# Two transformer blocks on one core: a row maximum taken from two neighbouring PSUM banks at once, score banks cut from three to two, and the products with the values moved into the middle of a step

## The chip, the cores and the metric

The kernel runs on one core of a Trainium2 chip. TensorE multiplies, VectorE, ScalarE and GpSimd work on what it makes, SyncE issues most transfers. TensorE writes into PSUM, which has eight banks of 512 float32 per partition; a bank can be written again when its reader is done. The metric is the device time of one execution in microseconds (us), taken as the median of several runs. Lower is better.

## The reference

Four sequences of 1024 tokens with 512 features pass two layers. Layer 0 is a block with conditioned layer norm, 16 heads of 32 with rotary embedding, and a feed-forward of 2048; layer 1 has 16 query heads on 4 key heads, no rotary, and gates. The heart of both:

```python
scores = jnp.einsum('bhqd,bhkd->bhqk', q, k) / np.sqrt(HD)
attn = jax.nn.softmax(scores, axis=-1)
out = jnp.einsum('bhqk,bhkd->bhqd', attn, v)
x = residual + out @ wo + bo
h = _ada_norm(x, cond, ln2_g, ln2_b, ada2_w, ada2_b)
ff = jax.nn.gelu(h @ ff_w1 + ff_b1, approximate=False) @ ff_w2 + ff_b2
return residual + ff
```

## The kernel before, in words

The program handles eight "batches" i in a row: the four sequences through layer 0 (i = 0 to 3), then through layer 1 (4 to 7). Each has an attention stage and a feed-forward stage. Each engine has its own instruction list, written out by hand, and the lists meet at counted semaphores.

An attention stage has 8 blocks (a group of four heads by 512 queries). Softmax needs each query's maximum over 1024 keys. It is computed ahead, in a pass of its own: for each of a block's 16 tiles (128 queries of one head), two matmuls of 512 keys ("halves", `max_item` of TensorE, L907) write a bank each, and VectorE reduces each bank to a column (L1476). After 32 halves a second small reduction joins the two columns of each tile (L1481), TensorE transposes them (L934), and a transfer puts them, negated, beside the queries as one more row, so that the later score matmul yields scores minus maximum. The maxima of block n + 1 are made while block n is used.

An attention stage is issued in 64 steps (8 for each block), followed by two steps that only finish. A step has
- four scores (`score`, L969): keys on partitions, 512 queries in a bank, which ScalarE turns into probabilities by an exponential (L1157);
- four halves of maxima for a later block, up to step 54 (there is no ninth block);
- the values (`values`, L986): four float32 matmuls with 32 columns of TensorE's array each (two passes, so eight instructions), over the probabilities of two steps earlier;
- in 30 of the steps, the totals (`totals`, L1001): the same form with ones, for the softmax's sums. Before it GpSimd adds two units of probabilities (`add_probs`, L702); an exponential waits until the sum that reads its slot six units earlier is done;
- in some steps a fill: a projection of keys, values or queries, an output projection, or a transpose for a layer norm.

Step s begins with a maximum; maxima and scores alternate; values and, where due, totals stand at the end (`attention` of TensorE, L1005). A score w goes to bank w modulo 3 and waits for exponential w - 3. Maxima and fills share banks 3, 6 and 7 in the attention stage, 6 and 7 elsewhere. A small planner at import (`pass_through`) deals them out: the least recently used allowed bank, whose next writer waits for the last reader (`bank_free`). Values accumulate in bank 4, totals in bank 5.

The last eight steps of an attention stage (the tail) have no maxima. The feed-forward has 33 iterations with 24 matmuls of 512 columns each (L806 to L808); from iteration 21 on, the next batch's first block of maxima is made between them. Before batch 0 there is a prologue, in which TensorE runs that same list of fills and maxima without a feed-forward around it.

ScalarE and VectorE also split weights into two half-precision parts in batches 0 to 3 (`split_high`, L1183, `split_low`, L1526), copy out the accumulated values and totals at fixed exponentials of a block (`O_AT`, `D_AT`), and finish a block two blocks later (`HI_AT`); GpSimd's part of it is placed by `LO_AT`.

## Time and profile before

| | |
|---|---|
| median of 3 runs | 4044.38 us (4036.17 to 4044.77) |
| the profiled execution | 4039.97 us, its span 4038.1 us |
| TensorE busy | 3800.2 us, 94% |
| VectorE busy | 2466.3 us, 61% |
| ScalarE busy | 1603.3 us, 40% |
| GpSimd busy | 1711.6 us, 42% |
| granted TensorE clock, mean | 0.975 |

The profile is that of one execution. A matmul's end is modelled and overlaps the next one's start, so the pace of TensorE is read from the distances of starts. A wait is put down to the instruction whose semaphore came last. "Granted clock" is the share of TensorE's full 2.4 GHz.

### The profile page before, as it was taken

What the parts mean: (1) busy time and instruction counts of PE and PEld (TensorE: products, weight loads), DVE (VectorE), ACT (ScalarE), POOL (GpSimd) and SP (SyncE); (2) the same over time, 40 slices, a digit from 0 to 9 for tenths busy, and PEclk for the clock granted to TensorE, in tenths of its full rate; (3) what the DMA queues carried; (4) which work ended last, traced back from release to release, by engine and by line L of the source; (5) the groups of instructions that cost most, each with busy time, mean ns of one, the idle gap of its engine ahead of it and who ended that gap; (6) DMA issues with size and microseconds to landing.
All of it is one profiled execution on the core that took longest, in us unless ns stands there. A gap on an engine that the chain in (4) does not pass through costs nothing.

```text
span 4038.1 us, 53506 instructions
## 1 busy us (share of the span) xinstructions
PE 3800.2 (94%) x20400; PEld 1502.4 (37%) x20400; DVE 2466.3 (61%) x3903; ACT 1603.3 (40%) x2807; POOL 1711.6 (42%) x955
## 2 busy tenths in 40 slices
PE   6988899998999989999899998999899998999999
PEld 4322344333543335433254323432244333533244
DVE  4687645765457755576555777367664776467742
ACT  1365312653125632155421653136511563136521
POOL 2376412673216742066510664037510673126620
PEclk9899999999999999999999999999999999999999
DMA  4232243212423223332233022311222112311122
GB/s 143 52 99 91 97 106 86 71 54 82 107 78 81 59 74 89 100 82 59 85 100 94 17 62 69 111 40 25 82 80 90 30 38 79 113 53 25 61 66 94
DMA packets 138973, 305.21 MB, mean 76 GB/s; under 512 B 19632, under 2 KB 59588, under 8 KB 137824
## 3 DMA queue, kind: packets, MB, share of 16 engines
q10 hardware_dynamic: 50944, 174.62, 13.4%
q1 hardware_dynamic: 87776, 127.17, 12.1%
q8 instruction: 164, 2.69, 0.3%
q14 instruction: 89, 0.73, 0.1%
HBM read 223.46 MB, written 36.66 MB: 64 GB/s over the span
## 4 chain that ended last, share of the span: by engine, by line
PE 80%; DVE 9%; POOL 4%; issue 3%; ACT 3%; DMA 1%; SPq 0%; ACTq 0%; POOLq 0%; DVEq 0%
PE ps L806 12%; PE ps L807 12%; PE ps L808 12%; PE ps L986 10%; PE ps L907 9%; PE ps L969 8%; PE ps L843 7%; PE ps L1001 5%; DVE mcol L1476 3%; PE ps L860 2%; POOL sums L702 2%; ACT probs L1157 2%; DVE ring L1526 2%; PE ps L824 1%; DVE dcopy L1493 1%
## 5 line engine op out<-in xcount | busy, mean ns | idle before, releaser
L702 POOL TENSOR_TENSOR sums<-probs 128x1024 f32<-128x1024 f32 x496 | 1175.6, 2384 | 1039.5 <-PE ps L1001 570.0
L1476 DVE TENSOR_REDUCE mcol<-ps 128x1 f32<-128x512 f32 x2048 | 1289.4, 682 | 454.0 <-PE ps L907 451.6
L1157 ACT ACTIVATE probs<-ps 128x512 f32<-128x512 f32 x2048 | 1098.9, 607 | 854.0 <-PE ps L969 617.6
L907 PE MATMUL ps<-ks,qs 97*128 97x512 f16 x2048 | 790.6, 388 | 64.4 <-DVE mcol L1476 47.0
L969 PE MATMUL ps<-qs,ks 98*128 98x512 f16 x2048 | 776.6, 389 | 77.4 <-ACT probs L1157 73.0
L1302 ACT ACTIVATE sums<-ps,cols 128x512 f32<-128x512 f32 x256 | 175.9, 687 | 1153.9 <-PE ps L808 1153.9
L986 PE MATMUL ps<-probs,v_sb 128*32 128x512 f32 x4096 | 568.0, 631 | 0.0
L907 PEld LDWEIGHTS ps<-ks,qs 97*128 97x128 f16 x2048 | 199.7, 98 | 624.9 <-DVE mcol L1476 375.2
L806 PE MATMUL ps<-ring,probs 128*128 128x512 f16 x1024 | 390.8, 382 | 20.6 <-DVE probs L1572 20.6
L806 PE MATMUL ps<-aT,ring 128*128 128x512 f16 x1024 | 388.3, 379 | 6.5 <-ACT dcopy L1169 6.5
L807 PE MATMUL ps<-ring,probs 128*128 128x512 f16 x1024 | 390.3, 381 | 0.0
L808 PE MATMUL ps<-ring,probs 128*128 128x512 f16 x1024 | 389.9, 381 | 0.0
L807 PE MATMUL ps<-aT,ring 128*128 128x512 f16 x1024 | 388.2, 379 | 0.0
L808 PE MATMUL ps<-aT,ring 128*128 128x512 f16 x1024 | 388.0, 379 | 0.0
L969 PEld LDWEIGHTS ps<-qs,ks 98*128 98x128 f16 x2048 | 198.0, 98 | 381.2 <-ACT probs L1157 247.5
L1571 DVE CAST probs<-sums 128x512 f16<-128x512 f32 x256 | 132.9, 519 | 305.7 <-ACT sums L1302 305.7
L843 PE MATMUL ps<-hT,wqkv 128*128 128x512 f16 x1248 | 297.3, 382 | 5.2 <-DVE wqkv L1646 5.2
L1001 PE MATMUL ps<-sums,ones 128*32 128x512 f32 x2048 | 280.6, 621 | 0.0
L687 POOL TENSOR_TENSOR turn<-turn 128x512 f32<-128x512 f32 x32 | 41.0, 1281 | 548.5 <-DVE turn L1410 548.5
L1572 DVE TENSOR_TENSOR probs<-sums,probs 128x512 f16<-128x512 f32 x256 | 207.4, 810 | 8.8
L1410 DVE SCALAR_TENSOR_TENSOR turn<-ps,bias,trig 128x512 f32<-128x512 f32 x128 | 89.9, 746 | 166.0 <-PE ps L843 149.7
L843 PEld LDWEIGHTS ps<-hT,wqkv 128*128 128x128 f16 x1248 | 120.8, 98 | 161.1 <-DVE mcol L1476 11.1
(106 smaller groups left out, 3273.7 us busy)
## 6 DMA issues: line engine op xcount, KB each, us to landing
ring<-halves ACTq DMA_DIRECT2D x208, 512.0 KB, 3.4
qs<-hl SPq DMA_DIRECT2D x192, 128.0 KB, 4.0
ring<-halves SPq DMA_DIRECT2D x48, 512.0 KB, 6.4
ring<-in_weights ACTq DMA_DIRECT2D x39, 512.0 KB, 4.3
halves<-ring ACTq DMA_DIRECT2D x37, 512.0 KB, 2.9
ks<-hl SPq DMA_DIRECT2D x120, 128.0 KB, 4.4
dcopy<-inverses SPq DMA_DIRECT2D x56, 256.0 KB
probs<-in_x SPq DMA_DIRECT2D x8, 1024.0 KB, 6.9
```

The source lines that it names most:

```text
L702: pool.tensor_tensor(sums[:, m % SUM_SLOTS, :, :], prob(u - 2), prob(u), ALU.add).then_inc(sum_set[0].sem, 1)
L806: pe.matmul(dst, lhs[0], rhs[0], start=first, stop=False)
L807: pe.matmul(dst, lhs[0], rhs[1], start=False, stop=False)
L808: return pe.matmul(dst, lhs[1], rhs[0], start=False, stop=last)
L843: mm = pe.matmul(bank, qkv(lw, weight_at(kind, i, hh, part, c), P), hT[:, lx, c, tok], start=(q == 0), stop=(q == 11))
L907: pe.matmul(bank, qs[0:K_MAX, hh, h, P * qt:P * qt + P], ks[0:K_MAX, key_set(i, hh), key_head(i, hh, h), 512 * half:512 * half + 512], sta ...
L969: pe.matmul(ps[:, bank, :], ks[0:K_EXP, key_set(i, hh), key_head(i, hh, h), P * kt:P * kt + P], qs[0:K_EXP, hh, h, :], start=True, stop=Tr ...
L986: mm = pe.matmul(ps[32 * q:32 * q + 32, 4, :], values_of(i, hh)[:, kt, value_cut(i, hh, 4 * g + q)], prob(u + q // 2)[:, q % 2, :], start= ...
L1001: mm = pe.matmul(ps[32 * q:32 * q + 32, 5, :], ones32[:, :], sums[:, (m + q // 2) % SUM_SLOTS, q % 2, :], start=(m % 8 == 0), stop=(m % 8 ...
L1157: act.activation(prob(u)[:, e, :], ps[:, w % SCORE_BANKS, :], ACT.Exp).then_inc(exp_done.sem, 1)
L1476: dve.tensor_reduce(mcol[:, blk % 2, 4 * j + qt, half:half + 1], src, AX.X, ALU.max).then_inc(n_free[0], 1)
L1572: dve.tensor_tensor(fT[:, n % 4, 1, :], g32[:, n % 2, :], fT[:, n % 4, 0, :], ALU.subtract).then_inc(f_set.sem, 1)
```

## The change

- Two halves of a tile go to two neighbouring banks, and VectorE takes one maximum over 1024 keys from both. The second small reduction and its buffer go. A block has 16 items of two halves; two items are issued in a step, as four halves were.
- The banks: scores 2 (0 and 1) instead of 3; maxima and fills 2, 3, 6, 7. An item takes a pair, (2, 3) or (6, 7); a fill takes a single bank of the four. In the feed-forward stage and the prologue there is only the pair (6, 7). Two banks, 2 and 3, now pass between the attention stage and the outputs of the feed-forward.
- In a step TensorE's order becomes: half 0, score 0, half 1, values, score 1, (first part of a fill), score 2, (second part), halves 2 and 3, score 3, and totals at the end where due.
- Small moves: the copy of totals from exponential 12 to 11 of a block, the finish from 11 to 15, GpSimd's part of it from sum 1 to 3; the parts of a weight split one to two exponentials or one step later, its store later too; one rotation's high part.
- In the feed-forward two items an iteration from 21 on (one from 27 on), the first ahead of the second matmul of the feed-forward, the other behind it.

```diff
@@ -30,19 +30,20 @@
 SCORES = 2 * UNITS
-SCORE_BANKS, MAX_BANKS, LATER_BANKS = 3, (3, 6, 7), (6, 7)
+SCORE_BANKS, MAX_BANKS, LATER_BANKS = 2, (2, 3, 6, 7), (6, 7)
+PAIRS = (2, 6)
 LAG = 4
 PROBS, SUM_SLOTS, SUMS = 6, 3, 64
-O_AT, D_AT, HI_AT, INVERT_AT, NORM_AT, LO_AT = 7, 12, 11, 4, 6, 1
+O_AT, D_AT, HI_AT, INVERT_AT, NORM_AT, LO_AT = 7, 11, 15, 4, 6, 3
 RING = 6
...
 L0_CHUNKS, L1_CHUNKS = 24, 21
-MAX_AT = (4, 6, 8, 10, 12, 14, 16, 18, 20, 22, 24, 26, 28, 30, 32)
-MAX_AT_K = (0, 2, 5, 7, 9, 11, 14, 16, 18, 20, 23, 25, 27, 29, 32)
+MAX_AT = (2, 4, 6, 8, 10, 12, 14, 16)
+MAX_AT_K = (0, 2, 4, 7, 9, 11, 14, 16)
 WO_AT = 52
...
 BIAS_AT = (49, 49, 50, 51, 53, 54, 55, 56)
-TURNS = ((("k", 1, 0), -1, 1, 5), (("k", 1, 1), 3, 3, 10), (("q", 0, 1), 11, 13, 29), (("q", 1, 1), 25, 27, 57))
+TURNS = ((("k", 1, 0), -1, 1, 5), (("k", 1, 1), 3, 3, 11), (("q", 0, 1), 11, 13, 29), (("q", 1, 1), 25, 27, 57))
@@ -54,19 +55,20 @@
-def max_step(i, u):
-
-    blk, s = divmod(u, 16)
-    if s < 14:
+def maxima_at(i, s):
+
+
+    blk, r = divmod(s, 8)
+    if r < 7:
         at = MAX_AT_K if layer(i) == 0 and blk == 1 else MAX_AT
-        items = [(blk + 1, k) for k in range(at[s], at[s + 1])]
+        items = [(blk + 1, k) for k in range(at[r], at[r + 1])]
     else:
-        items = [] if layer(i) == 0 and blk == 0 else [(blk + 2, k) for k in range(2 * (s - 14), 2 * (s - 13))]
-    return [(n, k) for n, k in items if n < 8]
+        items = [] if layer(i) == 0 and blk == 0 else [(blk + 2, k) for k in range(2)]
+    return [("max", i, n, k) for n, k in items if n < 8]
...
 def max_tile(k):
-    return k // 2 % 4, k // 8, k % 2
+    return k % 4, k // 4
@@ -141,13 +139,13 @@
         keys += [key for at, key in first_fills(j) if at == n]
-        first = {21: 0, 22: 4, 23: 8, 24: 11, 25: 14, 26: 17, 27: 20, 28: 23, 29: 26, 30: 29}
+        first = {21: 0, 22: 2, 23: 4, 24: 6, 25: 8, 26: 10, 27: 12, 28: 13, 29: 14, 30: 15}
         if n in first:
-            keys += [("max", j, 0, k) for k in range(first[n], first.get(n + 1, 32))]
+            keys += [("max", j, 0, k) for k in range(first[n], first.get(n + 1, 16))]
+        if n in (31, 32):
+            keys += [("max", j, 1, n - 31)]
         if n == 31:
             keys += [("rows", j, 0)]
-        if n in (31, 32):
-            keys += [("max", j, 1, 2 * (n - 31)), ("max", j, 1, 2 * (n - 31) + 1)]
     return keys
@@ -171,31 +169,45 @@
+
 NARROW, BANK, USER_BEFORE, FREED, LAST_USER = {}, {}, {}, {}, {}
...
 def pass_through(key, banks):
-    bank = [b for b in recent_ if b in banks][0]
-    recent_.remove(bank)
-    recent_.append(bank)
-    NARROW[key], BANK[key], USER_BEFORE[key] = len(NARROW), bank, LAST_USER.get(bank)
-    LAST_USER[bank] = key
+    if key[0] == "max":
+        _, bank = min((max(recent_.index(b), recent_.index(b + 1)), b) for b in PAIRS if b in banks)
+        used = (bank, bank + 1)
+    else:
+        bank = [b for b in recent_ if b in banks][0]
+        used = (bank,)
+    before = []
+    for b in used:
+        recent_.remove(b)
+        recent_.append(b)
+        if b in LAST_USER and LAST_USER[b] not in before:
+            before.append(LAST_USER[b])
+        LAST_USER[b] = key
+    NARROW[key], BANK[key], USER_BEFORE[key] = len(NARROW), bank, before
     read_[by_scalar(key)] += 1
...
-THIRD_FIRST, THIRD_LAST = {}, []
+SHARED_FIRST, SHARED_LAST = {}, []
 for i_ in range(-1, NB):
...
         keys_ = [key_ for s_ in range(STEPS) for key_ in narrow_attention(i_, s_)]
+        first_, last_ = {}, {}
         for key_ in keys_:
             pass_through(key_, MAX_BANKS)
-        third_ = [key_ for key_ in keys_ if BANK[key_] == 3]
-        THIRD_FIRST[third_[0]] = i_
-        THIRD_LAST.append(third_[-1])
+            for b_ in (2, 3):
+                if LAST_USER.get(b_) == key_:
+                    first_.setdefault(b_, key_)
+                    last_[b_] = key_
+        SHARED_FIRST.update({key_: i_ for key_ in first_.values()})
+        SHARED_LAST.append(list(dict.fromkeys(last_.values())))
     for n_ in range(FC * 2 + 1):
@@ -808,11 +818,10 @@
             def bank_free(key):
-                before = USER_BEFORE[key]
-                if before is not None:
+                for before in USER_BEFORE[key]:
                     pe.wait_ge(*freed(before))
-                if key in THIRD_FIRST and THIRD_FIRST[key] >= 1:
-                    pe.wait_ge(y_read.sem, y_read.at(THIRD_FIRST[key]))
+                if SHARED_FIRST.get(key, 0) >= 1:
+                    pe.wait_ge(y_read.sem, y_read.at(SHARED_FIRST[key]))
                 return ps[:, BANK[key], :]
@@ -896,17 +905,28 @@
-            def max_item(key):
+            def max_item(key, half):
+
                 _, i, blk, k = key
                 hh, qc, g = block_of(blk)
-                if k == 0:
-                    stacks_ready(i, blk)
-                bank = bank_free(key)
-                j, qt, half = max_tile(k)
+                if half == 0:
+                    if k == 0:
+                        stacks_ready(i, blk)
+                    bank_free(key)
+                j, qt = max_tile(k)
                 h = 4 * g + j
-                pe.matmul(bank, qs[0:K_MAX, hh, h, P * qt:P * qt + P],
-                          ks[0:K_MAX, key_set(i, hh), key_head(i, hh, h), 512 * half:512 * half + 512],
-                          start=True, stop=True).then_inc(n_full, 1)
+                mm = pe.matmul(ps[:, BANK[key] + half, :], qs[0:K_MAX, hh, h, P * qt:P * qt + P],
+                               ks[0:K_MAX, key_set(i, hh), key_head(i, hh, h), 512 * half:512 * half + 512],
+                               start=True, stop=True)
+                if half == 1:
+                    mm.then_inc(n_full, 1)
+
+            def max_halves(keys):
+                return [(key, half) for key in keys for half in range(2)]
+
+            def some_halves(halves):
+                for key, half in halves:
+                    max_item(key, half)
@@ -930,13 +950,13 @@
                 bank = bank_free(key)
-                pe.wait_ge(max_col.sem, max_col.at(i, blk + 1))
-                pe.transpose(bank[0:16, 0:P], mfin[:, :], ident[:, :]).then_inc(n_full, 1)
+                pe.wait_ge(*freed(("max", i, blk, 15)))
+                pe.transpose(bank[0:16, 0:P], mcol[:, blk % 2, :], ident[:, :]).then_inc(n_full, 1)
...
                 if kind == "max":
-                    max_item(key)
+                    some_halves(max_halves([key]))
                 elif kind == "rows":
@@ -1005,24 +1025,24 @@
                     u = 2 * s
+                    halves, fills = max_halves(maxima_at(i, s)), FILLS[i].get(s, [])
                     if s < STEPS:
-                        maxima, fills = maxima_at(i, s), FILLS[i].get(s, [])
-                        some(maxima[0:1])
+                        some_halves(halves[0:1])
                         score(i, 4 * s)
-                        some(maxima[1:2])
+                        some_halves(halves[1:2])
+                    if LAG <= u < UNITS + LAG:
+                        values(i, u - LAG)
+                    if s < STEPS:
                         score(i, 4 * s + 1)
...
                             fill(key, 0, 6 if key[0] in "kqv" else 12)
-                        some(() if fills else maxima[2:3])
                         score(i, 4 * s + 2)
...
                                 fill(key, 6, 12)
-                        some(maxima[2:3] if fills else maxima[3:4])
+                        some_halves(halves[2:4])
                         score(i, 4 * s + 3)
-                        some(maxima[3:] if fills else maxima[4:])
-                    if LAG <= u < UNITS + LAG:
-                        values(i, u - LAG)
+                        some_halves(halves[4:])
                     if s == STEPS + 1:
@@ -1061,7 +1081,8 @@
                             pe.wait_ge(exp_done.sem, exp_done.at(i, SCORES))
-                            pe.wait_ge(*freed(THIRD_LAST[i]))
+                            for key in SHARED_LAST[i]:
+                                pe.wait_ge(*freed(key))
                         for t in range(4):
@@ -1268,9 +1287,9 @@
                     for q, (st, ch) in enumerate(here):
-                        if u == 2 * st:
+                        if u == 2 * st + 1:
                             split_high(i, q)
-                        if u == 2 * st + 4:
+                        if u == 2 * st + 7:
                             store_split(i, q)
@@ -1471,14 +1490,14 @@
                 _, i, blk, k = key
-                j, qt, half = max_tile(k)
-                src = bank_full(key)
-                dve.tensor_reduce(mcol[:, blk % 2, 4 * j + qt, half:half + 1], src, AX.X, ALU.max).then_inc(n_free[0], 1)
+                j, qt = max_tile(k)
+                bank_full(key)
+                src = ps[:, BANK[key]:BANK[key] + 2, :].rearrange("p a d -> p (a d)")
+                at_ = 4 * j + qt
+                dve.tensor_reduce(mcol[:, blk % 2, at_:at_ + 1], src, AX.X, ALU.max).then_inc(n_free[0], 1)
...
                 _, i, blk = key
-                dve.wait_ge(*freed(("max", i, blk, 31)))
-                dve.tensor_reduce(mfin[:, :], mcol[:, blk % 2, :, :], AX.X, ALU.max).then_inc(max_col.sem, 1)
                 src = bank_full(key)
@@ -1549,9 +1568,9 @@
                     for q, (st, ch) in enumerate(here):
-                        if s == st:
+                        if s == st + 1:
                             split_low(i, q, 0)
-                        if s == st + 1:
+                        if s == st + 2:
                             split_low(i, q, 1)
...
```

TensorE in step 40 of batch 4, before: L907 is a half of a maximum, L969 a score, L986 the values, L1001 the totals; in brackets what each waits for (exp_done: exponentials; n_free: VectorE's reader).

```order
L907 MATMUL ps<-ks,qs 128x512 [waits n_free]
L969 MATMUL ps<-qs,ks 128x512 [waits exp_done,max_in]
L907 MATMUL ps<-ks,qs 128x512 [waits n_free]
L969 MATMUL ps<-qs,ks 128x512 [waits exp_done]
L907 MATMUL ps<-ks,qs 128x512 [waits n_free]
L969 MATMUL ps<-qs,ks 128x512 [waits exp_done]
L907 MATMUL ps<-ks,qs 128x512 [waits n_free]
L969 MATMUL ps<-qs,ks 128x512 [waits exp_done]
L986 MATMUL ps<-probs,v_sb 32x512 [waits exp_done]
L986 MATMUL ps<-probs,v_sb 32x512 x3
L1001 MATMUL ps<-sums,ones 32x512 [waits sum_set0]
L1001 MATMUL ps<-sums,ones 32x512 x3
```

The same step after; L918 is a half, L989 a score, L1006 the values, L1021 the totals.

```order
L918 MATMUL ps<-ks,qs 128x512 [waits n_free]
L989 MATMUL ps<-qs,ks 128x512 [waits exp_done,max_in]
L918 MATMUL ps<-ks,qs 128x512
L1006 MATMUL ps<-probs,v_sb 32x512 [waits exp_done]
L1006 MATMUL ps<-probs,v_sb 32x512 x3
L989 MATMUL ps<-qs,ks 128x512 [waits exp_done] x2
L918 MATMUL ps<-ks,qs 128x512 [waits n_free]
L918 MATMUL ps<-ks,qs 128x512
L989 MATMUL ps<-qs,ks 128x512 [waits exp_done]
L1021 MATMUL ps<-sums,ones 32x512 [waits sum_set0]
L1021 MATMUL ps<-sums,ones 32x512 x3
```

The values have moved from before the totals to behind the first score, so the step has two places with 32-column matmuls, and the second half of an item waits for nothing.

TensorE at the end of the prologue, before: value projections (L860), the 32 halves of block 0, the transpose (L934), and the first halves of block 1.

```order
L860 MATMUL ps<-wqkv,hT 128x256 [waits n_free,s_rows]
L860 MATMUL ps<-wqkv,hT 128x256 x23
L907 MATMUL ps<-ks,qs 128x512 [waits mask_in0,stack_in0,n_free]
L907 MATMUL ps<-ks,qs 128x512 [waits n_free] x31
L934 MATMUL ps<-ident,mfin 16x128 [waits max_col,n_free]
L907 MATMUL ps<-ks,qs 128x512 [waits mask_in0,stack_in0,n_free]
L907 MATMUL ps<-ks,qs 128x512 [waits n_free] x3
```

The same place after (L869 is the projection, L918 a half):

```order
L869 MATMUL ps<-wqkv,hT 128x256 [waits n_free,s_rows]
L869 MATMUL ps<-wqkv,hT 128x256 x23
L918 MATMUL ps<-ks,qs 128x512 [waits mask_in0,n_free,stack_in0]
L918 MATMUL ps<-ks,qs 128x512
L918 MATMUL ps<-ks,qs 128x512 [waits n_free]
L918 MATMUL ps<-ks,qs 128x512
L918 MATMUL ps<-ks,qs 128x512 [waits n_free]
```

Every second half is now preceded by a wait for a reader; all these items have the one pair of banks 6 and 7, where before two single banks were filled in turn.

## Rows read from the trace of the kernel before

**Rows 1.** The page, part 1: busy us, share of the span, instructions.
```profile
PE 3800.2 (94%) x20400; PEld 1502.4 (37%) x20400; DVE 2466.3 (61%) x3903; ACT 1603.3 (40%) x2807; POOL 1711.6 (42%) x955
```

**Rows 2.** TensorE's waits: us, times, longest; whole run, then batch 0 (129:436).
```profile
PE ps L969 <- ACT probs L1157: 73.0, 110, 9.0
PE ps L907 <- DVE mcol L1476: 47.0, 59, 2.2
...
PE ps L934 <- DVE mfin L1481: 10.2, 17, 1.8
...
PE ps L907 <- DVE mcol L1476: 20.7, 15, 2.2
```

**Rows 3.** Windows (batch 4, steps 40-47; tail): us; busy PE, PEld, DVE, ACT, POOL; clock.
```profile
2353.40:2380.20 26.80, 26.51 (x163) 7.97 (x162) 20.72 (x35) 18.12 (x36) 21.06 (x11) 1.00 0.03 11
2415.40:2453.00 37.60, 29.13 (x158) 8.44 (x160) 21.56 (x22) 21.20 (x41) 20.98 (x12) 0.86 0.24 89
```

**Rows 4.** Timeline of TensorE, batch 4, steps 37 and 38: start, duration.
```profile
2342.73 1.04 PE L1001 MATMUL ps<-sums,ones 128*32 128x512 f32 x8
2343.70 0.39 PE L907 MATMUL ps<-ks,qs 97*128 97x512 f16 x1
...
2345.24 0.38 PE L969 MATMUL ps<-qs,ks 98*128 98x512 f16 x1
2345.55 1.06 PE L986 MATMUL ps<-probs,v_sb 128*32 128x512 f32 x8
2346.55 0.39 PE L907 MATMUL ps<-ks,qs 97*128 97x512 f16 x1
...
2348.39 1.06 PE L986 MATMUL ps<-probs,v_sb 128*32 128x512 f32 x8
2349.28 1.04 PE L1001 MATMUL ps<-sums,ones 128*32 128x512 f32 x8
2350.25 0.28 PE L934 MATMUL ps<-ident,mfin 128*16 128x128 f32 x1
```

**Rows 5.** The same stretch on ScalarE, GpSimd and VectorE.
```profile
2346.42 3.04 ACT L1157 ACTIVATE probs<-ps 128x512 f32<-128x512 f32 x6 [0.99 <-POOL sums L702]
...
2343.95 4.67 POOL L702 TENSOR_TENSOR sums<-probs 128x1024 f32<-128x1024 f32 x2 [0.75 <-PE ps L1001]
...
2344.13 2.48 DVE L1476 TENSOR_REDUCE mcol<-ps 128x1 f32<-128x512 f32 x4 [0.77 <-PE ps L907]
```

**Rows 6.** Tail of batch 2: timeline of TensorE, then of ScalarE.
```profile
1435.23 0.82 PE L969 MATMUL ps<-qs,ks 98*128 98x512 f16 x3
1436.31 0.39 PE L969 MATMUL ps<-qs,ks 98*128 98x512 f16 x1 [0.26 <-ACT probs L1157]
...
1445.56 0.61 PE L969 MATMUL ps<-qs,ks 98*128 98x512 f16 x1 [3.59 <-ACT probs L1157]
...
1435.66 2.07 ACT L1157 ACTIVATE probs<-ps 128x512 f32<-128x512 f32 x4 [0.45 <-PE ps L969]
...
1444.91 1.08 ACT L1157 ACTIVATE probs<-ps 128x512 f32<-128x512 f32 x2 [4.21 <-POOL sums L702]
```

**Rows 7.** The page, part 5: draining a rotated projection on VectorE.
```profile
L1410 DVE SCALAR_TENSOR_TENSOR turn<-ps,bias,trig 128x512 f32<-128x512 f32 x128 | 89.9, 746 | 166.0 <-PE ps L843 149.7
```

**Rows 8.** Timeline of ScalarE in batch 2: a split of weights.
```profile
1278.05 1.09 ACT L1183 ACTIVATE ring<-ring 128x1024 f16<-128x1024 f32 x1
```

**Rows 9.** Timeline of TensorE in the prologue.
```profile
106.97 1.21 PE L907 MATMUL ps<-ks,qs 97*128 97x512 f16 x2 [0.18 <-DVE mcol L1476]
108.36 1.21 PE L907 MATMUL ps<-ks,qs 97*128 97x512 f16 x2 [0.18 <-DVE mcol L1476]
```

18 lines of the change are left out of this document (6 added, 12 removed).

## The prediction

> **What bounds the kernel now.** I read the page's busy times first: TensorE is busy 94% of the span, VectorE 61% and ScalarE 40% [rows 1]. Its waits sum to little: 73.0 us for exponentials (ScalarE has not yet emptied a score bank), 47.0 us for maxima (VectorE), 10.2 us for the small reduction ahead of the row transposes [rows 2]. The windows then show where they lie. Steps 40 to 47 of batch 4 last 26.8 us, with TensorE busy 26.51 us at full clock; the last eight steps, which have no maxima, last 37.6 us with 29.13 us busy, at a clock of 0.86 [rows 3]. So seven eighths of an attention stage of the second layer run at the rate at which TensorE issues, and there a change can only lose; what can be gained lies in the tails, in batch 0 (20.7 us of waits for maxima, [rows 2]) and a little in batches 1 to 3.
>
> "Busy" hides short waits, since a 0.38 us matmul overlaps the next, which starts 0.22 us later. So the pace is read from starts [rows 4]. An odd step lasts 2343.70 to 2346.55 = 2.85 us: four scores and four maxima in turn, seven distances of (2345.24 - 2343.70)/7 = 0.22, then 0.31 from the last score to the values and 1.00 from the values to the next matmul. An even step lasts to 2350.25 = 3.70 us: values to totals 0.89, totals onward 0.97. A pair is 6.55 us.
>
> **1. Values in mid-step: one more switch.** Before, values and totals of an even step are neighbours. A matmul of 128 columns is followed by the next after 0.22, but by values after 0.31; values are followed by totals after 0.89, but by a half-precision matmul after 1.00 [rows 4]. With values between score 0 and score 1, and totals still at the end, each even step has both edges twice: 0.09 + 0.11 = 0.20 us more. The order rows show the two separate visits. 30 totals per batch stand in steps, 240 in all, so 48 us if nothing hides it; the five per batch that lie in the waiting tail count for nothing here. The Trainium skill, TensorEngine Tiling (Array Packing), Key Properties, says that a change of tiling mode drains TensorE; values and totals are 32-column tiles. The trace agrees that each such edge costs, and it is a rule against this change; the sum takes 0.20 us from the rows.
>
> **2. Two score banks.** Score w now waits for exponential w-2, not w-3. A score at 1435.23 has its exponential at 1435.66, 0.43 later; the fourth score from there waited for the first one's bank and started at 1436.31, 0.65 after that exponential [rows 6]. So two scores of one bank cannot start closer than 1.08 us. Before, three banks asked this of scores six matmuls (1.3 us) apart. After, score 1 and score 3 have only score 2 and two halves between them, 4 x 0.22 = 0.88: a wait of 0.20 in every step without a fill, which holds up all that stands behind it on TensorE (totals, the next item), and through it VectorE and ScalarE, which idle there. Score 0 and score 2 have the values between them and are safe.
> Score 0 of the next step needs the exponential of score 2. GpSimd decides that one after a step with totals: totals at 2342.73, exponential released by the sum at 2346.42, 3.69 later [rows 4, 5], bank free at 4.34. The score is due at 0.97 + odd step 3.05 + 0.22 = 4.24: a wait of 0.10. Here 3.05 = 0.22 + 0.22 + 0.31 + 1.00 + 1.08 + 0.22.
> The even step becomes 0.22 + 0.22 + 0.31 + 1.00 + 1.08 + 0.31 + 0.97 = 4.11. The pair is 4.11 + 3.05 + 0.10 = 7.26 against 6.55: +0.71, in which the switch of part 1 is contained. None of it shows as much idle time: waits of 0.1 to 0.2 us lie under the modelled 0.38 us.
> Steps 2 to 51 without a fill: 46 in each batch of layer 1, 38 in batches 1 to 3, 40 in batch 0, together 338, or 169 pairs. 169 x 0.71 = **120 us**. Its bounds: 34 us (169 x 0.20, if waits for score banks vanish under other waits) and 135 us (0.80 a pair, if ScalarE is late as well). I take 120, since batch 4's rows leave nothing else to hide it.
> Outside those pairs 31 switches in fill steps add 31 x 0.20 = +6 us. In tails the same two-bank rule gives an odd step without maxima 0.31 + 1.00 + 1.08 + 0.48 = 2.87 (0.48: the second exponential starts half a microsecond behind the first); before, 0.31 + 1.00 + 3 x 0.22 = 1.97 was possible. But the tail waits for GpSimd: one of its sums let an exponential through at 1444.91 only, and TensorE waited 3.59 us [rows 6]. TensorE's slower steps mostly eat that wait: +5 us for eight batches (0 to +25).
>
> **3. One maximum over 1024 keys.** 2048 reductions of 0.68 us (four in 2.48 us back to back, so 0.60 each, [rows 5]) become 1024. One of twice the length costs between 0.68 and 1.20; I take 1.20, as the time should grow with the elements. VectorE loses little work; what counts is the bank cycle: the reduction starts about 0.43 after the second half, ends 1.20 later. In the attention two pairs alternate, an item per pair and step, against steps of 3 us: no wait. In the feed-forward only banks 6 and 7, one pair, are left, but 2.6 us of matmuls stand between items: no wait either. Two places lack that cover.
> The prologue issues 16 items in a row. Before: pairs of halves every 1.39 us (106.97 to 108.36), the pace of VectorE [rows 9]. After, TensorE writes two halves, waits for the whole reduction and starts again: 0.22 + 0.43 + 1.20 + 0.05 = 1.9 us at full clock, and about 2.4 with matmuls at twice the distance, as this stretch seems to have them (its matmuls last 0.61 us on average where others last 0.38). 16 x (2.3 - 1.39) = +15 us (8 to 20). And in step 21 of the feed-forward ahead of batches 1 to 3 a value projection and two items come in one run behind each other on that pair: 3 x 2.4 = +7 us.
> A fill takes a bank of the pair that the next step's first item needs, with 4 x 0.22 of cover in an odd step instead of 2 us; its drain takes 0.43 plus two operations of 0.75 [rows 7]. About 1 us in seven fill steps of each early batch and two of each late one, less about as much that batches 0 to 3 already wait: +12 us.
>
> **4. ScalarE's and VectorE's other work.** Splits of weights (1.09 us each on ScalarE, [rows 8]), the two-part finishes of a block and the copies now stand at other exponentials and meet one bank less of cover. A split between two exponentials delays the second by 1.1 us, and score 2, two places behind it, has 1.75 us less 1.08 to spare: 39 splits and 24 finishes at 0.2 us on average: +12 us (0 to 25). First steps 0 and 1 of a batch: +5 us.
> On the other side the splits' second halves move a step later on VectorE, and it no longer waits for ScalarE between reductions. I give back 30 of the 47.0 us of waits for maxima, 5 of the 10.2 us ahead of the row transposes, as that reduction is gone [rows 2], and 5 us of clock in batch 0: -40 us.
>
> **Sum.** 120 + 6 + 5 + 15 + 7 + 12 + 12 + 5 - 40 = +142 us on the profiled execution's 4040.0 us: 4182. The runs' median is 4.4 us above that execution: **4186 us**, 3.5% slower.
>
> **The rivals.**
> A. The short waits are hidden after all (exponentials sooner than the two rows say, or the score wait overlaps the array switch), and only the switches cost: 34 + 6 for them, and the other terms as they are: 120 becomes 34, +56 us, 4100. For it: no row of before has a score whose bank was used two scores ago. Against: the 0.43 and 0.65 are the way from score to exponential and back, whichever bank it is.
> B. The idle slivers bring the clock down. The tail of batch 4, busy 77%, ran at 0.86 [rows 3]. If the 338 steady steps ran at 0.95 instead of 1.00, their 169 x 7.26 = 1227 us would grow by 5%: +65 us more, 4251. Against: in the new pair TensorE waits only 0.50 of 7.26 us. The Trainium skill, TensorE: Matmul & The Clock Gate, A second HAM failure mode, describes this of PSUM banks cycled with small idles; no row here shows it in the steady steps.
> C. Faster. Values issued ahead of scores 1 to 3 free the probability slots earlier, VectorE is no longer late, and TensorE stops waiting for both: all 73.0 + 47.0 + 10.2 us go [rows 2] and two-bank waits do not appear, against 48 us of switches: -82 us, 3962. It decides if exponentials in the tails are released by values, not by GpSimd's sums. Against: the releaser of the long wait is the sum [rows 6], and the steady steps have nothing to give.
> D. Gains and losses cancel within 0.2% (8 us, about what a measurement of this kernel can tell from no change): 4044.
>
> **How the numbers follow.** The forecast has 0.72, A 0.12, B 0.09, C 0.04, D 0.03. Slower: 0.72 + 0.12 + 0.09 = 0.93; same 0.03, faster 0.04. The range must leave out no more than 0.2: with the bounds of the terms (the tail, prologue, fills and ScalarE's other work together -25 to +45 around the sum, the 120 down to 34) it is 4095 to 4265, which holds A and nearly B.
>
> **What would show it.** In the steady steps of batch 4: pairs of about 7.2 us by starts; values 0.31 after a maximum and 1.00 ahead of score 1; score 3 at 1.08 after score 1, its wait put down to ScalarE; totals with edges 0.31 and 0.97; the block of steps 40 to 47 near 29.5 us instead of 26.8, clock 1.00. The reduction near 1.2 us, 1024 of them. Prologue items 1.9 to 2.4 us apart. Fewer waits for maxima in batch 0. It would be wrong if steady pairs stay below 6.9 us, if the clock sinks there, or if the tails get shorter by more than a few us.

## The result: slower by 4.9%, and the profile after

The changed kernel takes 4238.05 us (median of 4 runs, 4235.68 to 4244.49) against 4043.1 us for the kernel before (median of 4 on the same chip): a ratio of 1.0488 (95% interval 1.0470 to 1.0506). The forecast was 4186 us, 3.5% slower, in a range of 4095 to 4265. The profiled execution took 4235.68 us, its span 4233.9, so 195.8 us more of span than before. The direction is as forecast and the time lies in the range, but the loss is 195 us where 142 were forecast.

The page of the changed kernel, engines and its longest reduction (L1497 is the maximum):

```profile
PE 3915.0 (92%) x20400; PEld 1444.2 (34%) x20400; DVE 2415.9 (57%) x2815; ACT 1680.1 (40%) x2807; POOL 1721.0 (41%) x955
...
L1497 DVE TENSOR_REDUCE mcol<-ps 128x1 f32<-128x1024 f32 x1024 | 1238.4, 1221 | 709.9 <-PE ps L918 708.9
```

TensorE's waits (L989 a score, L918 a half, L1006 the values, L954 the row transpose; us in total, times, longest), to be read beside [rows 2]:

```profile
PE ps L989 <- ACT probs L1176: 98.7, 142, 4.2
PE ps L954 <- DVE mcol L1497: 30.8, 27, 2.0
PE ps L918 <- DVE mcol L1497: 29.2, 25, 1.4
PE ps L1006 <- ACT ocopy L1182: 20.8, 43, 0.6
...
PE ps L918 <- DVE turn L1429: 17.1, 20, 0.9
...
PE ps L918 <- DMA ks<-hl: 8.8, 4, 2.8
PE ps L918 <- DVE hl L1438: 7.4, 8, 1.2
```

VectorE is less busy than before (2415.9 us), as intended, and TensorE waits longer. The ones for exponentials rose from 73.0 to 98.7 us and the ones ahead of the row transposes by 20.6, those for maxima fell from 47.0 to 29.2; most of the loss is not in this list. It is in the starts. Windows of batch 4, steps 40 to 47 and the tail, beside [rows 3]:

```profile
2463.70:2493.90 30.20, 29.34 (x162) 6.78 (x163) 20.23 (x19) 19.52 (x36) 21.21 (x11) 1.00 0.03 11
2531.00:2571.40 40.40, 31.86 (x168) 8.09 (x167) 20.91 (x23) 23.25 (x42) 21.88 (x13) 0.87 0.23 83
```

The block of eight steps went from 26.8 to 30.2 us at full clock, with 29.34 us "busy". The clock did not sink there, and on the whole it is 0.975 as before. TensorE's timeline there, steps 36 and 37 and the start of 38, beside [rows 4]:

```profile
2448.42 0.38 PE L918 MATMUL ps<-ks,qs 97*128 97x512 f16 x1
2448.73 0.39 PE L989 MATMUL ps<-qs,ks 98*128 98x512 f16 x1
2448.96 0.38 PE L918 MATMUL ps<-ks,qs 97*128 97x512 f16 x1
2449.27 1.06 PE L1006 MATMUL ps<-probs,v_sb 128*32 128x512 f32 x8
2450.27 0.61 PE L989 MATMUL ps<-qs,ks 98*128 98x512 f16 x2
2450.71 0.60 PE L918 MATMUL ps<-ks,qs 97*128 97x512 f16 x2
2451.35 0.39 PE L989 MATMUL ps<-qs,ks 98*128 98x512 f16 x1
2451.66 1.06 PE L1021 MATMUL ps<-sums,ones 128*32 128x512 f32 x8
2452.66 0.39 PE L918 MATMUL ps<-ks,qs 97*128 97x512 f16 x1
...
2455.72 0.38 PE L918 MATMUL ps<-ks,qs 97*128 97x512 f16 x1
2456.04 0.39 PE L989 MATMUL ps<-qs,ks 98*128 98x512 f16 x1
```

The reader is to see four distances. Values 0.31 after a half and 1.00 ahead of score 1 (2449.27, 2450.27); score 3 at 2451.35, exactly 1.08 after score 1, 0.20 behind where it could have stood; totals again 0.31 and 1.00; and at the start of step 38 the score at 2456.04, 0.32 instead of 0.22 after its half, the 0.10 us that GpSimd's late sum costs. From first score to first score the even step is 4.16, the odd one 3.14 to 3.15 us: a pair of 7.30, where 7.26 was forecast and 6.55 stood.

### The profile page after: what moved, and what is told of

Read it like the earlier page. It is cut to its first block, busy times and chain, and to the rows that moved or that the text cites. A ratio compares the mean times of both kernels' runs of the same rounds, so it can differ in the third digit from the quotient of the medians.

```text
span 4233.9 us, 52561 instructions
## 1 busy us (share of the span) xinstructions
PE 3915.0 (92%) x20400; PEld 1444.2 (34%) x20400; DVE 2415.9 (57%) x2815; ACT 1680.1 (40%) x2807; POOL 1721.0 (41%) x955
## 4 chain that ended last, share of the span: by engine, by line
PE 80%; DVE 7%; ACT 5%; POOL 4%; issue 3%; DMA 1%; ACTq 0%; SPq 0%; POOLq 0%; DVEq 0%
PE ps L816 12%; PE ps L818 11%; PE ps L817 11%; PE ps L989 10%; PE ps L1006 10%; PE ps L918 9%; PE ps L852 6%; PE ps L1021 5%; ACT probs L1176 3%; POOL sums L712 2%; DVE mcol L1497 2%; PE ps L869 2%; PE ps L833 1%; DMA ks<-hl 1%; DVE turn L1429 1%
## 5 line engine op out<-in xcount | busy, mean ns | idle before, releaser
L1497 DVE TENSOR_REDUCE mcol<-ps 128x1 f32<-128x1024 f32 x1024 | 1238.4, 1221 | 709.9 <-PE ps L918 708.9
L1176 ACT ACTIVATE probs<-ps 128x512 f32<-128x512 f32 x2048 | 1167.6, 596 | 935.8 <-PE ps L989 878.2
L989 PE MATMUL ps<-qs,ks 98*128 98x512 f16 x2048 | 747.3, 394 | 113.7 <-ACT probs L1176 98.7
L918 PE MATMUL ps<-ks,qs 97*128 97x512 f16 x2048 | 701.3, 389 | 81.2 <-DVE mcol L1497 29.2
L1006 PE MATMUL ps<-probs,v_sb 128*32 128x512 f32 x4096 | 561.5, 622 | 22.5 <-ACT ocopy L1182 20.8
L989 PEld LDWEIGHTS ps<-qs,ks 98*128 98x128 f16 x2048 | 173.5, 97 | 896.0 <-ACT probs L1176 736.6
L816 PE MATMUL ps<-ring,probs 128*128 128x512 f16 x1024 | 391.1, 382 | 20.6 <-DVE probs L1591 20.6
L918 PEld LDWEIGHTS ps<-ks,qs 97*128 97x128 f16 x2048 | 200.3, 99 | 425.8 <-DVE mcol L1497 148.3
L1021 PE MATMUL ps<-sums,ones 128*32 128x512 f32 x2048 | 280.7, 621 | 0.0
L852 PEld LDWEIGHTS ps<-hT,wqkv 128*128 128x128 f16 x1248 | 122.4, 98 | 151.7 <-issue 10.2
```

Source lines behind the costliest of these rows:

```text
L816: pe.matmul(dst, lhs[0], rhs[0], start=first, stop=False)
L852: mm = pe.matmul(bank, qkv(lw, weight_at(kind, i, hh, part, c), P), hT[:, lx, c, tok], start=(q == 0), stop=(q == 11))
L918: mm = pe.matmul(ps[:, BANK[key] + half, :], qs[0:K_MAX, hh, h, P * qt:P * qt + P], ks[0:K_MAX, key_set(i, hh), key_head(i, hh, h), 512 * ...
L989: pe.matmul(ps[:, bank, :], ks[0:K_EXP, key_set(i, hh), key_head(i, hh, h), P * kt:P * kt + P], qs[0:K_EXP, hh, h, :], start=True, stop=Tr ...
L1006: mm = pe.matmul(ps[32 * q:32 * q + 32, 4, :], values_of(i, hh)[:, kt, value_cut(i, hh, 4 * g + q)], prob(u + q // 2)[:, q % 2, :], start= ...
L1021: mm = pe.matmul(ps[32 * q:32 * q + 32, 5, :], ones32[:, :], sums[:, (m + q // 2) % SUM_SLOTS, q % 2, :], start=(m % 8 == 0), stop=(m % 8 ...
```

## Where the 195 us lie

Differences of the starts of scores, summed by kind of step over all batches (measured in both traces), against what the terms of the forecast gave to the same places. A tail is counted from the first score of step 56 to its last score; what follows, up to the next batch's first score, stands under the feed-forward stages.

| place | forecast | measured |
|---|---|---|
| steps without a fill, from the third to step 51 | 120 + 12 - 40 = 92 | 108.2 |
| steps with a fill (32.3), and 52 to 55 (14.2) | 6 + 12 = 18 | 46.5 |
| prologue | 15 | 15.3 |
| first two steps of a batch (batches 4 to 7 alone: 7.9) | 5 | 7.3 |
| tails | 5 | 10.4 |
| feed-forward stages | 7 | 8.0 |
| sum | 142 | 195.7 |

The first line by batches: batches 4 to 7 lose 76.5 us, batches 1 to 3 lose 36.2, and batch 0 gains 4.5.

## Experiments

Twelve kernels. A name that begins with b_ is the kernel before with an edit, one with a_ the changed kernel with an edit. Ratios are to the kernel before on the same chip. The changed kernel was timed on the chip of the result alone, where the kernel before took 4043.1 us; on the three chips of the experiments that took 4035.8 to 4037.7. So "faster than the changed kernel" is the difference of two losses, each against the kernel before on its own chip: 195 us for the changed kernel. The plain difference of the two medians is 5 to 7 us more.

### 1. Values in mid-step alone

```diff
 # TensorE, attention: kernel before
                         some(maxima[1:2])
+                    if LAG <= u < UNITS + LAG:
+                        values(i, u - LAG)
+                    if s < STEPS:
                         score(i, 4 * s + 1)
...
                         some(maxima[3:] if fills else maxima[4:])
-                    if LAG <= u < UNITS + LAG:
-                        values(i, u - LAG)
```

> The kernel before, with the values issued between the first and the second score of a step; three score banks, single banks for maxima. Theory (each separate visit of the 32-column matmuls costs about 0.20 us, 240 totals stand in steps): the even step of the second layer goes from 3.70 to 3.90 us, the odd one stays at 2.85, the whole is 40 to 48 us slower, about 4087 us. Rival (the switch is hidden, or values issued earlier free something): no change or faster, 4043 us or less.

Measured 4128.05 us, 1.0227 (1.0213 to 1.0241): +90 us, twice the forecast of the switch. TensorE in steps 37 and 38 of batch 4:

```profile
2392.01 0.39 PE L907 MATMUL ps<-ks,qs 97*128 97x512 f16 x1
...
2392.45 0.38 PE L907 MATMUL ps<-ks,qs 97*128 97x512 f16 x1
2392.76 1.06 PE L986 MATMUL ps<-probs,v_sb 128*32 128x512 f32 x8
2393.76 0.39 PE L969 MATMUL ps<-qs,ks 98*128 98x512 f16 x1
...
2395.30 0.38 PE L907 MATMUL ps<-ks,qs 97*128 97x512 f16 x1
```

The switch is what was forecast: the odd step is 2.85 (from the matmul ahead of the values, 2392.45, to the same one of the next step, 2395.30), the even one 3.94 against 3.70, +0.24, which over 200 steps is 48 us. The rest shows up in waits that the move uncovers (TensorE's waits in this kernel), beside [rows 2]:

```profile
PE ps L986 <- ACT ocopy L1164: 65.1, 44, 5.5
...
PE ps L934 <- DVE mfin L1482: 28.5, 25, 1.9
PE ps L969 <- ACT probs L1158: 23.7, 16, 9.3
...
PE ps L907 <- DVE turn L1411: 20.4, 24, 0.9
```

The values wait for the copy of their bank, 65.1 us in 44 waits; no such wait stood in the list of before. Not all of that is loss: 33.7 us of it are eight single waits, one in each tail, and the tails became 10 us shorter, as the waits for exponentials fell from 73.0 to 23.7 us. The row transposes wait 28.5 instead of 10.2 us, and a first maximum behind a rotated projection 20.4 us. At the end of a step the values' 1.3 us (0.31 and 1.00) had stood in front of all three. By steps: those with a fill lose 34.8 us and steps 52 to 55 another 20.1, their switches included. The theory of the switch stands, the theory that the switch is all falls.

### 2. Two score banks alone

```diff
-SCORE_BANKS, MAX_BANKS, LATER_BANKS = 3, (3, 6, 7), (6, 7)
+SCORE_BANKS, MAX_BANKS, LATER_BANKS = 2, (3, 6, 7), (6, 7)
```

> The kernel before with two score banks in turn instead of three (bank 2 idle in the attention stage), all else as before. Theory (two scores of one bank start at least 1.08 us apart, and the second exponential follows the first by 0.48): score 2 at 1.08 instead of 0.88 after score 0, score 3 at 1.56 instead of 1.32, so every steady step is 0.24 us longer, 2.85 to 3.09 and 3.70 to 3.94; 338 steps give +81 us, about 4125 us. Rival (the waits for score banks vanish under others): within 10 us of before.

Measured 4132.85 us, 1.0231 (1.0217 to 1.0245): +95 us. The steady steps of batch 4 are 3.14 odd and 3.96 even (3.09 and 3.94 expected), with one of 3.59 a block. They carry 77.5 of the 95 us; steps with fills and 52 to 55 lose 1.4 us together. This kernel's list of waits understates it:

```profile
PE ps L969 <- ACT probs L1157: 106.7, 169, 8.8
```

That is 34 us more than before, for a loss of 95: the remainder lies under the modelled ends of matmuls. The rival is out. Alone, the moved values and the two banks cost about 2.3% each; the whole change costs 4.9%.

### 3. Values back at the end of the step, two banks kept

```diff
 # TensorE, attention: changed kernel
                         some_halves(halves[1:2])
-                    if LAG <= u < UNITS + LAG:
-                        values(i, u - LAG)
-                    if s < STEPS:
                         score(i, 4 * s + 1)
...
                         some_halves(halves[4:])
+                    if LAG <= u < UNITS + LAG:
+                        values(i, u - LAG)
```

> The changed kernel with the values back at the end of a step, next to the totals; two score banks and the pairs stay. Theory (mid-step values cost a switch but cover a score bank): the second visit goes (-0.20 us in an even step), but score 2 now follows score 0 with 0.66 us between and must keep 1.08, so each step waits 0.42. By starts in the second layer's steady steps 3.27 odd and 4.12 even, a pair of 7.39 us against 7.28: that alone +19 us. The waits that appeared behind fills and ahead of the row transposes (values no longer cover VectorE) should go at the same time: about 1 us in seven fill steps of batches 0 to 3 and two to four of the others, and 0.2 to 0.5 us a block: -30 us. About 4225 us, 4205 to 4260. Rival (the switch is all that the move costs): pairs of 7.08 us and 4190 us or less.

Measured 4205.18 us, 1.0423 (1.0407 to 1.0439), 26 us faster than the changed kernel, twice the 13 expected. The steady steps came as worked out, 3.27 odd and 4.12 to 4.13 even (3.27 and 4.12 expected): worse than with values in mid-step. One even step a block takes 4.50, which nothing here explains. What got better is the steps with fills (-24.1 us) and 52 to 55 (-7.2). This time the waits for exponentials show in the list, as a steady step should wait 0.42 us:

```profile
PE ps L989 <- ACT probs L1175: 205.5, 424, 4.0
```

So with two banks values in mid-step are the better place in a steady step, and the worse one in a step with a fill. The rival (pairs of 7.08) is out.

### 4. Another order for the same two banks

```diff
+                    spaced = s < STEPS and halves and not fills and not rows_at(i, s)
                     if s < STEPS:
-                        some_halves(halves[0:1])
+                        some_halves([] if spaced else halves[0:1])
                         score(i, 4 * s)
-                        some_halves(halves[1:2])
+                        some_halves(halves[0:2] if spaced else halves[1:2])
+                        if spaced:
+                            score(i, 4 * s + 1)
                     if LAG <= u < UNITS + LAG:
                         values(i, u - LAG)
+                    for pair in range(SUMS // 2 - 2):
+                        if spaced and s == totals_step(i, pair):
+                            totals(i, 2 * pair)
                     if s < STEPS:
-                        score(i, 4 * s + 1)
+                        if not spaced:
+                            score(i, 4 * s + 1)
...
-                        if s == totals_step(i, pair):
+                        if not spaced and s == totals_step(i, pair):
                             totals(i, 2 * pair)
```

> The changed kernel, but steps that have maxima and neither a fill nor a row transpose are issued as score 0, half, half, score 1, values, totals, score 2, half, half, score 3. Theory (only distances between scores of one bank and visits of the 32-column matmuls set the pace): score 0 to 2 and 1 to 3 are covered by the values, score 2 to the next score 0 has 0.88 and needs 1.08, one visit an even step: odd 3.05, even 3.91 us, the pair 6.96 instead of 7.28; a block of steps 32 to 39 of the second layer about 28.5 instead of 30.1 us; 4180 us, 4170 to 4195. Rival (the number of score banks as such sets the pace, by ScalarE): pairs stay at 7.2 or more and the whole within 15 us of the changed kernel.

Measured 4161.97 us, 1.0308 (1.0294 to 1.0323), 69 us faster than the changed kernel; the time is below the 4170 to 4195 expected. The steps of batch 4 from 32 on: 3.89, 3.05, 4.16, 3.05, 3.91, 3.07, 4.08, 3.30, together 28.5 us, as forecast to the tenth. Step 36 and the start of 37:

```profile
2422.84 1.07 PE L1006 MATMUL ps<-probs,v_sb 128*32 128x512 f32 x8
2423.73 1.04 PE L1021 MATMUL ps<-sums,ones 128*32 128x512 f32 x8
2424.70 0.39 PE L989 MATMUL ps<-qs,ks 98*128 98x512 f16 x1
2424.93 0.60 PE L918 MATMUL ps<-ks,qs 97*128 97x512 f16 x2
2425.36 0.81 PE L989 MATMUL ps<-qs,ks 98*128 98x512 f16 x2
2426.01 0.60 PE L918 MATMUL ps<-ks,qs 97*128 97x512 f16 x2
```

Values and totals touch (0.89), one visit; score 2 at 2424.70, and the next score 0 is the second of the two from 2425.36, held by its bank until about 1.08 after score 2. The number of banks sets the pace only through the distance between two scores of one bank; the rival is out.

### 5. The length of the maximum

```diff
-                src = ps[:, BANK[key]:BANK[key] + 2, :].rearrange("p a d -> p (a d)")
+                src = ps[:, BANK[key]:BANK[key] + 2, :].rearrange("p a d -> p (a d)")[:, ::2]
...
-                dve.tensor_scalar(mT[:, :], src[0:16, 0:P], -1.0, None, ALU.mult).then_inc(n_free[0], 1)
+                dve.tensor_scalar(mT[:, :], src[0:16, 0:P], -1.0, -40.0, ALU.mult, ALU.add).then_inc(n_free[0], 1)
```

> The changed kernel with the maximum taken over every second of the 1024 keys only (half of the keys left out of the maximum, and 40 subtracted to keep the exponentials small), so that the instruction has 512 elements, as long as one of before. Theory (of the whole loss the length of the maximum is the small part: it delays the prologue's items, the row transposes and a few first maxima): reduction 0.68 us instead of 1.22, prologue 10 us shorter, the row transposes' 30.8 us and the maxima's 29.2 us of waits smaller by 20 us together; 25 to 35 us faster than the changed kernel, about 4208 us, and the steady pair still 7.28 us. Rival (the longer reduction is what slows the steady steps): pairs near 6.75 us and under 4120 us.

Measured 4197.74 us, 1.0397 (1.0383 to 1.0411), 34 us faster than the changed kernel. The steady pair did not move (4.15 and 3.14 us); the prologue is 8.9 us shorter, and of TensorE's waits the two for the maximum, 29.2 and 30.8 us in the changed kernel, are here

```profile
PE ps L918 <- DVE mcol L1497: 20.5, 30, 0.9
...
PE ps L954 <- DVE mcol L1497: 11.3, 17, 1.1
```

The longer reduction costs about a sixth of the loss, and nothing in the pairs that have neither fill nor transpose. The rival is out.

### 6. The prologue

```diff
-            pass_through(key_, LATER_BANKS)
+            pass_through(key_, LATER_BANKS if i_ >= 0 else MAX_BANKS)
```

> The changed kernel with both pairs of banks open to the prologue as well, where it has only the pair (6, 7). Theory (with one pair TensorE writes and VectorE reduces in turn, 2.3 us an item; with two they overlap, about 1.2 to 1.4 us an item): attention of batch 0 starts 12 to 16 us earlier and the whole is 12 to 16 us faster, about 4224 us. Rival (VectorE or the clock bounds the prologue): under 5 us.

Measured 4217.83 us, 1.0440 (1.0426 to 1.0454), 15 us faster. In the changed kernel, items follow each other after 2.35 us, beside [rows 9], and VectorE is busy for 1.22 of it only. Its TensorE (the distance of two items):

```profile
106.59 1.03 PE L918 MATMUL ps<-ks,qs 97*128 97x512 f16 x2 [1.32 <-DVE mcol L1497]
108.94 1.03 PE L918 MATMUL ps<-ks,qs 97*128 97x512 f16 x2 [1.32 <-DVE mcol L1497]
```

VectorE between them, in the same kernel:

```profile
107.66 1.22 DVE L1497 TENSOR_REDUCE mcol<-ps 128x1 f32<-128x1024 f32 x1 [1.13 <-PE ps L918]
```

TensorE in the experiment, with both pairs:

```profile
106.75 2.17 PE L918 MATMUL ps<-ks,qs 97*128 97x512 f16 x4 [0.19 <-DVE mcol L1497]
109.10 2.17 PE L918 MATMUL ps<-ks,qs 97*128 97x512 f16 x4 [0.19 <-DVE mcol L1497]
```

Four halves, two items, in 2.35 us. The first score comes 25.6 us earlier (12 to 16 expected). Of these, 17.6 us are the items themselves, now 1.18 us apart, VectorE's pace. Another 7.0 us lie ahead of them: the edit opens the banks to the prologue's projections too, and the first item starts at 95.3 instead of 102.3. About 10 of the 25.6 us are lost again later, mostly in attention steps (7 us); why stays open.

### 7. The copy of the values

The changed kernel, and the kernel before:

```diff
-O_AT, D_AT, HI_AT, INVERT_AT, NORM_AT, LO_AT = 7, 11, 15, 4, 6, 3
+O_AT, D_AT, HI_AT, INVERT_AT, NORM_AT, LO_AT = 6, 11, 15, 4, 6, 3
```

```diff
-O_AT, D_AT, HI_AT, INVERT_AT, NORM_AT, LO_AT = 7, 12, 11, 4, 6, 1
+O_AT, D_AT, HI_AT, INVERT_AT, NORM_AT, LO_AT = 8, 12, 11, 4, 6, 1
```

> The changed kernel with the copy of the accumulated values after exponential 6 of the next block instead of 7. Theory (43 waits of 0.48 us of the values for that copy, 20.8 us, exist because the values moved ahead of three scores while the copy did not move): these waits go, the step at s mod 8 = 2 falls from 4.74 to about 4.2 us, the whole by 15 to 22 us, to 4218 us. Rival (the copy ahead of exponential 7 delays it and with it a score by as much): within 6 us.

> The kernel before with the same copy after exponential 8 instead of 7. In its trace the step at s mod 8 = 2 takes 4.17 us instead of 3.70, since exponential 8, released late by GpSimd's sum, stands behind the copy, and score 3 waits for its bank. Theory: with the exponential first that wait shrinks to 0.1 us, 0.35 us in some 48 steps: -15 us, 4028 us. Rival (the values then wait for the copy by as much): within 4 us of before.

Measured 4219.87 us, 1.0455 (1.0439 to 1.0471), 11 us faster than the changed kernel (its span is 17 us shorter; 15 to 22 expected): the step at s mod 8 = 2 went from 4.74 to 4.20, and the 20.8 us of waits are gone but for 0.2. For the kernel before: 4027.91 us, 0.9980 (0.9971 to 0.9989): that step of the kernel before fell from 4.17 to 3.93 only, half of the forecast's gain.

### 8. The splits of weights

In the kernel before, the moves of the change; in the changed kernel, their undoing.

```diff
-                        if u == 2 * st:
+                        if u == 2 * st + 1:
                             split_high(i, q)
-                        if u == 2 * st + 4:
+                        if u == 2 * st + 7:
...
-                        if s == st:
+                        if s == st + 1 :
                             split_low(i, q, 0)
-                        if s == st + 1:
+                        if s == st + 2:
```

> The kernel before with only the weight splits moved as the change moves them (ScalarE's half after exponential 4s+3 instead of 4s+1, VectorE's halves one step later, the store three units later). Theory (VectorE then no longer stands waiting for ScalarE ahead of the maxima): the waits of 1.8 us in batch 0 go, 20 us there with some clock, a few us in batches 1 to 3; 4015 to 4028 us. Rival (the waits only move, or the gain of batch 0 in the changed kernel came from the longer maximum): within 8 us of before.

> The changed kernel with the weight splits back at the places of the kernel before. Theory (moved late, VectorE's part falls beside GpSimd's sums and ahead of maxima that are due, as the kernel before with late splits showed at steps 7 and 15 of batches 0 to 3): earlier splits take 2 us from each of blocks 0 and 3 to 6 us from each of blocks 1 of batches 0 to 3, 15 to 30 us in all, about 4215 us; batches 4 to 7, which have none, stay. Rival (with two score banks and the longer maximum the late places are the better ones, as the moves were made together): the same or slower, 4238 us or more, batch 0 above all.

Measured 4074.48 us, 1.0088 (1.0074 to 1.0101): 37 us slower, where a gain of 8 to 20 was expected. In batches 0 to 3, block 0 lost 1.0 to 2.4 and block 1 lost 4.0 to 6.3 us. The loss of block 0 lies between the first scores of steps 7 and 8: the first maximum of step 8 waits for the transfer that completes the next keys (`ks<-hl`), 7.9 us in 4 waits, against 0.3 us before. Step 15 of batch 2 of b_splits_late, first VectorE's timeline:

```profile
1284.54 2.62 DVE L1526 SCALAR_TENSOR_TENSOR ring<-ring 128x512 f16<-128x512 f32 x1
```

GpSimd's timeline beside it:

```profile
1284.26 2.34 POOL L702 TENSOR_TENSOR sums<-probs 128x1024 f32<-128x1024 f32 x1 [0.21 <-PE ps L1001]
```

And TensorE's, behind them:

```profile
1287.82 0.42 PE L907 MATMUL ps<-ks,qs 97*128 97x512 f16 x1 [2.17 <-DVE mcol L1476]
```

VectorE's part takes 0.68 us when GpSimd is idle (median of 19) and 1.5 us when GpSimd works all the while (median of 29, the longest 2.8); here one piece of 2.62 us stands beside a sum and ahead of maxima that TensorE needs. In the changed kernel the undoing gave 4237.12 us, 1.0492 (1.0476 to 1.0508), the same as the changed kernel within the intervals, where 15 to 30 us were expected: 10 us less in block 0 of all batches, somewhat more elsewhere. The wait for the keys is in the changed kernel as well, 8.8 us in 4 waits, and shrinks to 0.6 with the splits early; so this part of the late splits costs the same in both kernels. The 4 to 6 us of block 1 do not come back, and why was not settled.

### 9. Together, and the best version

> The changed kernel with three of the mends together: the spaced order of steps, both pairs of banks in the prologue, the copy of values after exponential 6. Theory (they act at different places and add up): 4162 us of the spaced order, less 20 for the prologue, less 0.25 us in 48 steps for the copy: 4130 us, 4120 to 4140, still slower than the kernel before, since its steady pair is 6.96 against 6.55 us. Rival (GpSimd's sums or ScalarE take over as the bound): within 10 us of 4162.

Spaced order, both pairs in the prologue, the early copy: 4139.21 us, 1.0250 (1.0236 to 1.0264). The mends took half of the loss, 93 us of 195, and the time lies within the expected band (4120 to 4140). That the rest is all the two banks' was not shown.

> The kernel before with the copy of values after exponential 8 and with banks 3, 6 and 7 open to the prologue. Theory: with three banks VectorE takes the 32 maxima of the prologue back to back, 0.60 us each, 19 us instead of 22: 3 us on top of the 8 us of the late copy; 4025 us, ratio 0.9965 to 0.998 of before. Rival (the clock bounds the prologue): the same as with the late copy alone.

The kernel before with the late copy and three banks in the prologue: 4021.41 us, 0.9959 (0.9947 to 0.9972), 0.4% faster than the kernel before and a little better than the 0.9965 to 0.998 expected. The prologue became 7.5 us shorter, where 3 were expected: 3.2 us in the maxima, as worked out, and 4.3 ahead of them, where the projections use the third bank as well.

## Why the prediction was right, and what it sized wrongly

**Part 1, the switch.** Right to the hundredth in its distances (0.31, 1.00, [rows 4]); alone it adds 0.24 us to an even step (experiment 1), 0.20 forecast. The Trainium skill's rule that a change of tiling mode drains TensorE (TensorEngine Tiling (Array Packing), Key Properties) fits: each further visit cost these 0.24 us. The rows show the price, not its reason.

**Part 2, two banks.** Right: 1.08 us between scores of one bank, 0.10 for GpSimd's sum, pairs of 7.30 against 7.26; and experiments 3 and 4 placed the same 1.08 in two other orders and met their plain steps within 0.02 us, but for the one of 4.50 in experiment 3. What was too small is 0.71 as the mean of all pairs. A block of the second layer has four: two grew by 0.74 and 0.75, the one with the copy of the values by 0.87, the one with the row transpose by 0.96. Over the 92 pairs of batches 4 to 7 the term gives 65 us, and 76.5 were measured. The copy has no term in the forecast, yet held the values in 43 places (20.8 us); it did little harm in the sum only because that step of the kernel before was already long, 4.17 instead of 3.70.

**Part 3, the maximum.** 1.22 us against 1.20 taken. The prologue's 15 us and the feed-forward's 7 came as they should. The step of the forecast that was sized wrongly is the fills. "About 1 us in seven fill steps ... less about as much that batches 0 to 3 already wait" gave 12 us (18 with the switches there), and 46.5 were measured. Step 13 of batch 4, TensorE's timeline in the kernel before:

```profile
2254.59 1.46 PE L843 MATMUL ps<-hT,wqkv 128*128 128x512 f16 x6
...
2256.33 0.38 PE L907 MATMUL ps<-ks,qs 97*128 97x512 f16 x1
2256.64 1.07 PE L986 MATMUL ps<-probs,v_sb 128*32 128x512 f32 x8
2257.64 0.39 PE L907 MATMUL ps<-ks,qs 97*128 97x512 f16 x1
```

The same step in the changed kernel, TensorE:

```profile
2353.88 1.46 PE L852 MATMUL ps<-hT,wqkv 128*128 128x512 f16 x6
2355.18 0.60 PE L918 MATMUL ps<-ks,qs 97*128 97x512 f16 x2
2355.61 0.38 PE L989 MATMUL ps<-qs,ks 98*128 98x512 f16 x1
2356.88 0.39 PE L918 MATMUL ps<-ks,qs 97*128 97x512 f16 x1 [0.89 <-DVE hl L1438]
```

And VectorE there, the drain of the fill:

```profile
2356.13 0.69 DVE L1438 SCALAR_TENSOR_TENSOR hl<-ps,hl 128x512 f16<-128x512 f32 x1 [3.66 <-ACT hl L1150]
```

Before, half, score and half follow the fill, the last of them at 2256.33; then come the values, and the next step's half starts at 2257.64 without a wait. After, the values are gone from there; the drain begins at 2356.13, and the next step's half waits until 2356.88, 0.89 us. The step grew from 5.44 to 6.50. It takes 6.50 in experiment 1 too, with single banks and short maxima, and 5.43 in experiment 3, with pairs and the values back at the end: here the moved values did it, not the pairs, on which the forecast put it ("a fill takes a bank of the pair"). For all these places the same holds in the main. The moved values alone cost 55 us there (experiment 1), and putting them back gave 31 of the 46.5 back (experiment 3), 7 of these in the output projections of steps 52 to 55, which the forecast left out and which cost 14.2. Another 8.9 us lie in step 7 of batches 0 to 3, where the wait for the keys stands that comes with the late splits (experiment 8). The cost of a fill was forecast for a few steps only, and less "about as much that batches 0 to 3 already wait"; batches 0 to 3 still lost 29 us in these steps.

**Part 4, the give-back of 40 us.** The second term that was sized wrongly. Of the 47.0 us of waits for maxima 18 went instead of 30, all of them in batch 0 (20.7 to 2.7). Batch 0's steps without fills ended 4.5 us shorter where two banks alone should have cost 20 x 0.71 = 14: about 19 us were gained. Batches 1 to 3 gained some 4. The waits ahead of the row transposes were to shrink by 5 us and grew by 20.6 (10.2 to 30.8): the small reduction is gone, but the values no longer stand between the last maximum and the transpose, and that maximum takes 1.22 us (with one of 0.68 us they were 11.3, experiment 5). The cause given for batch 0, the late splits, falls: by themselves they cost 37 us and left 18.9 of the 20.7 us of waits, and with the splits early the changed kernel keeps the gain (1.6 us of waits). The moved values alone bring these waits to 9.4 us and two banks alone to 14.5, both with the splits as before; two banks alone made blocks 4 and 5 of batch 0 shorter by 3.0 and 2.5 us. That a slower pace of TensorE is what lets VectorE catch up fits this, but no run shows it by itself. So the gain in batch 0 was forecast for a cause that is not its own. The +12 us for ScalarE's other work were never measured apart.

**The rivals.** A (waits hidden) is out by experiment 2, B (the clock) by the windows, C and D by the time.

So the mechanism was right and the sum 53 us too small: 28 in steps with fills and 52 to 55, 16 in the other steps (the pairs with a transpose or a copy, and a give-back that was too large), 5 in tails and a small rest.

## What to carry to other kernels

Before work is moved away from the end of a step, list what its time covers there: here the same 1.3 us stood in front of a bank's copy, a drain and a reduction, and each came back as a wait. With n banks in turn, take from the trace the time from one writer to the next writer of the same bank, and count the slots of the issue order between them; an order that spreads them gave 69 us back here with the same two banks (0.34 us a pair), where taking the third bank away cost 95. A shorter reduction on VectorE, busy 57 to 61% beside a TensorE at 92 to 94%, bought nothing in the steady steps (experiment 5).

## What the runs showed of the hardware

- A matmul of 128 columns followed by 32-column ones starts them 0.31 us later instead of 0.22. On the way back, the next 128-column matmul starts 1.00 us after the eight of 32 columns; the next group of 32 columns starts after 0.88 to 0.89.
- From the start of a 512-column matmul to the start of a reader that is free 0.41 to 0.43 us, and from the exponential's start to the next writer of the bank, where that waits for it, 0.65 (0.63 at least): 1.07 to 1.08 us between two writers, in every order tried (the result, experiments 2 to 4).
- One reduction over two banks takes 1.22 us, against 0.68 over one; back to back 1.18 (experiment 6) against 2 x 0.60 [rows 5]: the saving in VectorE's time is small.
- A float32 pass over SBUF on VectorE took 0.68 us with GpSimd idle and often longer beside GpSimd's work: a median of 1.5 us and up to 2.8 in experiment 8's first kernel, but 0.85 (median of 24) in the changed kernel, some at 0.62. Working side by side did not always slow it, and what decides was not tested.
